# Four-layer cross-attention kernel: the second attention's exponential takes negated maxima as a bias, layer 0's scores use a second ring of banks, and the places of the last layer's stages change

## The reference

```python
# layer 0: per sequence, instance norm, two 64x64 projections, one softmax over the channels' pairs
A  = softmax(Mn^T Mm, axis=-1);  x = Wo (Ml A^T) + bo + x
# layer 1 (the first attention): 32 query heads on 8 key heads, 64 keys, head size 8, additive mask
x  = layernorm(softmax(q k^T / sqrt(8) + mask) v @ Wo + bo + x) * gamma + beta
# layer 2 (the second attention): latents x, keys from context and latents: 128 keys, 16 heads of size 16
a  = softmax(where(mask, q k^T / 16, -inf), axis=-1)
x  = gelu(rmsnorm((a v) @ out_w + out_b + x) @ mlp_w1 + b1) @ mlp_w2 + b2 + x
# layer 3: a recurrent block; per head a state s of 8x8 over 64 time steps, and a channel mix
s  = k_t v_t + w_t * s;  out_t = r_t (u k_t v_t + s)
```

## Time and profile before

| what | value |
|---|---|
| profiled execution, its own time | 1816.85 us |
| its span, first to last instruction | 1815.0 us |
| median of three other executions | 1815.32 us (1812.19 to 1816.52) |
| mean granted TensorE clock | 0.959 of full speed |
| busy: PE, DVE, ACT, POOL | 89%, 67%, 52%, 42% |
| period of a group (group 3's layer 0 to group 4's) | 623.52 to 840.90 us |

### The profile page before, as it was taken

How to read it: one execution, slowest core, us unless ns; L and a number is a source line. 1 busy time by engine, 2 the same in 40 slices (tenths; PEclk the granted TensorE clock), 3 DMA queues, 4 the chain that set the end, 5 groups by cost and what they waited for, 6 DMA issues and landing times.

```text
span 1815.0 us, 35492 instructions
## 1 busy us (share of the span) xinstructions
PE 1621.3 (89%) x13831; PEld 1053.9 (58%) x13831; DVE 1221.7 (67%) x2259; ACT 936.1 (52%) x1922; POOL 770.9 (42%) x882
## 2 busy tenths in 40 slices
PE   5888898899998899998998989889899889988856
PEld 3666556675565655655566655667456565565534
DVE  3743569755786558845689456975579665884496
ACT  4455545555645545556455564555564554555313
POOL 5532248603584046721477024860358404672000
PEclk8999999998999999999999999999999999999978
DMA  6001014210241004310061101421024100520060
GB/s 194 1 2 38 1 18 56 32 36 7 33 58 37 19 1 57 40 30 19 1 72 26 30 20 18 55 34 34 7 35 56 37 20 1 62 36 1 13 90 17
DMA packets 75924, 60.84 MB, mean 34 GB/s; under 512 B 39264, under 2 KB 60912, under 8 KB 75760
## 3 DMA queue, kind: packets, MB, share of 16 engines
q1 hardware_dynamic: 58000, 47.99, 18.3%
q10 hardware_dynamic: 17216, 10.55, 2.1%
q0 software_dynamic: 544, 0.03, 0.0%
HBM read 20.28 MB, written 4.19 MB: 13 GB/s over the span
## 4 chain that ended last, share of the span: by engine, by line
PE 66%; DVE 14%; ACT 9%; issue 5%; POOL 5%; DMA 0%; ACTq 0%; DVEq 0%; SPq 0%; POOLq 0%
PE bank L690 26%; PE bank L834 7%; PE bank L1097 6%; PE bank L1034 5%; DVE late L1409 4%; PE bank L706 3%; PE bank L1059 2%; PE bank L981 2%; ACT soft_ring L1235 2%; PE bank L967 2%; POOL soft_ring L1785 2%; PE bank L1052 2%; PE bank L943 2%; PE bank L954 1%; PE bank L774 1%
## 5 line engine op out<-in xcount | busy, mean ns | idle before, releaser
L1785 POOL TENSOR_TENSOR soft_ring<-soft_ring,seg_max 128x512 f32<-128x512 f32 x256 | 279.5, 1107 | 282.4 <-DVE seg_max L1575 281.4
L1250 ACT ACTIVATE soft_ring<-soft_ring 128x512 f32<-128x512 f32 x256 | 160.1, 625 | 188.1 <-POOL soft_ring L1785 188.0
L1409 DVE TENSOR_TENSOR_SCAN late<-late 128x520 f32<-128x520 f32 (+1 forms) x128 | 211.1, 1649 | 15.8 <-POOL late L1740 12.2
L834 PE MATMUL bank<-early 32*128 32x128 f32 (+2 forms) x1024 | 152.3, 416 | 39.1 <-ACT soft_ring L1235 37.9
L1034 PE MATMUL bank<-ident,soft_ring 128*128 128x128 f32 x1024 | 165.0, 290 | 22.8 <-ACT soft_ring L1250 17.4
L1738 POOL TENSOR_TENSOR late<-late 128x520 f32<-128x520 f32 x112 | 167.9, 1499 | 38.9 <-DVE late L1409 38.5
L1034 PEld LDWEIGHTS bank<-ident,soft_ring 128*128 128x128 f32 x1024 | 116.9, 145 | 92.8 <-ACT soft_ring L1250 44.9
L1575 DVE TENSOR_REDUCE seg_max<-soft_ring 128x8 f32<-128x512 f32 (+1 forms) x256 | 165.5, 674 | 0.2
L1751 POOL COPY late<-edge 128x8 f32<-128x8 f32 (+1 forms) x16 | 3.1, 197 | 327.2 <-DVE late L1513 279.5
L1793 POOL TENSOR_SCALAR soft_ring<-soft_ring,rden 128x256 f32<-128x256 f32 x64 | 59.3, 927 | 180.4 <-DVE rden L1537 180.4
L834 PEld LDWEIGHTS bank<-early 32*128 32x128 f32 (+1 forms) x1024 | 76.7, 192 | 90.0 <-issue 88.0
(11 more groups left out here) (327 smaller groups left out, 3482.2 us busy)
## 6 DMA issues: line engine op xcount, KB each, us to landing
late<-late SPq DMA_DIRECT2D x112, 260.0 KB, 4.4
c<-in_ctx ACTq DMA_DIRECT2D x8, 512.0 KB, 4.1
x<-in_x ACTq DMA_DIRECT2D x8, 512.0 KB, 4.9
out_x<-late SPq DMA_DIRECT2D x7, 512.0 KB, 2.9
late<-late SPq DMA_DIRECT2D x16, 130.0 KB, 3.8
early<-early SPq DMA_DIRECT2D x16, 130.0 KB, 3.6
mask<-in_mask_Bx1xSxS_ff ACTq DMA_DIRECT2D x16, 128.0 KB, 4.0
mask<-in_mask_BxS_ik SPq DMA_DIRECT2D x8, 256.0 KB, 3.5
```

What stands on the lines that cost most here:

```text
L834: ins = mm(t[:, width * n:width * n + width], lhsT, rhs, start=True, stop=True)
L1250: af(soft[:, u % SOFT, :], soft[:, u % SOFT, :], ACT.Exp).then_inc(sig("exp"), 1)
L1409: nc.vector.tensor_tensor_scan(P.sj[:, n % 2, :], P.wP[:, k, :, :].rearrange("p b t -> p (b t)"), P.aj[:, n % 2, :], 0.0, ALU.mult, ALU.ad ...
L1785: tt(s, s, seg_max[:, u % SOFT, 0:segs].unsqueeze(2).broadcast_to([128, segs, 512 // segs]), ALU.subtract).then_inc(sig("sub"), 1)
```

## The change

It has five parts. Maxima of the second attention are written negated, POOL no longer subtracts them, and ACT takes four exponentials of 128 columns with a column of the maxima as bias, in place of one of 512; ACT waits for DVE's "max" where it waited for POOL's "sub". In layer 0 the scores of pairs 1 and 3 go to the ring "turn". The two squares of a half (L1302) are waited for once and not one by one. `PLACES` and `SCAN_PLACES` have new numbers (in the order PE, ACT, DVE, POOL).

```diff
-            "normalize": (4, 12, 1, 0),
-            "turn": (11, 12, 5, 0),
-            "shift": (12, 15, 11, 4),
-            "maa": (15, 16, 12, 12),
-            "mix 0": (17, 29, 16, 18),
-            "mix 1": (22, 29, 20, 18),
+            "normalize": (4, 5, 1, 0),
+            "turn": (11, 10, 3, 0),
+            "shift": (11, 10, 11, 9),
+            "maa": (15, 15, 15, 10),
+            "mix 0": (17, 28, 18, 17),
+            "mix 1": (22, 28, 24, 28),
...
-            "bonus": (56, 49, 54, 56),
-            "center": (124, 124, 121, 113),
-            "variance": (127, 128, 122, 121),
-            "gate": (132, 130, 124, 121),
-            "project": (132, 133, 126, 127),
+            "bonus": (56, 50, 53, 54),
+            "center": (125, 125, 121, 118),
+            "variance": (127, 127, 124, 126),
+            "gate": (130, 129, 124, 126),
+            "project": (133, 133, 124, 126),
...
-            "ffn k": (135, 135, 133, 141),
-            "ffn r": (141, 145, 137, 147),
-            "ffn v": (149, 151, 148, 151),
+            "ffn k": (135, 141, 128, 138),
+            "ffn r": (138, 149, 128, 153),
+            "ffn v": (147, 154, 146, 156),
         }
         SCAN_PLACES = (
-            (64, 53, 64, 60), (64, 53, 68, 63), (64, 54, 68, 66), (64, 59, 69, 67), (72, 59, 69, 67),
-            (78, 78, 69, 67), (78, 80, 70, 67), (84, 88, 84, 70), (85, 91, 88, 89), (98, 93, 88, 89),
-            (101, 93, 100, 89), (107, 93, 105, 100), (112, 94, 108, 105), (116, 94, 109, 107), (116, 97, 114, 109),
-            (116, 107, 117, 109), (116, 109, 117, 109), (116, 111, 119, 111), (122, 114, 121, 111),
+            (63, 52, 64, 58), (63, 54, 67, 65), (64, 54, 67, 66), (65, 61, 67, 67), (71, 61, 69, 67),
+            (75, 79, 69, 67), (75, 79, 71, 67), (83, 89, 83, 67), (83, 90, 88, 85), (96, 93, 88, 89),
+            (100, 93, 100, 90), (105, 99, 106, 100), (109, 100, 108, 105), (112, 102, 109, 105), (112, 102, 115, 105),
+            (112, 106, 117, 105), (116, 107, 120, 110), (116, 110, 120, 110), (125, 115, 121, 110),
         )
...
-                def side_by_side(tiles, steps, operands):
-                    held = [fill(pe, "score", tile) for tile in tiles]
+                def side_by_side(tiles, steps, operands, ring="score"):
+                    held = [fill(pe, ring, tile) for tile in tiles]
...
                     side_by_side([("s0", 2 * p), ("s0", 2 * p + 1)], 2, lambda n, half: (
-                        mn[HALVES[half], p, 128 * n:128 * n + 128], mm0[HALVES[half], p, :]))
+                        mn[HALVES[half], p, 128 * n:128 * n + 128], mm0[HALVES[half], p, :]), "turn" if p % 2 else "score")
...
                 def exps(u):
                     tables(LOG_EXP, TANH)
-                    act.wait_ge(sig("sub"), past("sub") + u + 1)
-                    af(soft[:, u % SOFT, :], soft[:, u % SOFT, :], ACT.Exp).then_inc(sig("exp"), 1)
+                    if u < UNITS:
+                        act.wait_ge(sig("sub"), past("sub") + u + 1)
+                        af(soft[:, u % SOFT, :], soft[:, u % SOFT, :], ACT.Exp).then_inc(sig("exp"), 1)
+                        return
+                    act.wait_ge(sig("max"), past("max") + u + 1)
+                    s = soft[:, u % SOFT, :].rearrange("p (h n) -> p h n", h=4)
+                    for h in range(4):
+                        ins = af(s[:, h, :], s[:, h, :], ACT.Exp, bias=seg_max[:, u % SOFT, h:h + 1])
+                    ins.then_inc(sig("exp"), 1)
...
-                                link(af(xh[:, p, :], xr[:, p, :], ACT.Square, accum_out=stats[:, p, 0:1]))
+                                ins = af(xh[:, p, :], xr[:, p, :], ACT.Square, accum_out=stats[:, p, 0:1])
+                            link(ins)
...
                     nc.vector.tensor_reduce(seg_max[:, u % SOFT, 0:KVH if u < UNITS else 4], cuts(u, soft[:, u % SOFT, :]),
-                                            X, ALU.max).then_inc(sig("max"), 1)
+                                            X, ALU.max, negate=u >= UNITS).then_inc(sig("max"), 1)
...
                 def subtract(u):
                     pool.wait_ge(sig("max"), past("max") + u + 1)
-                    segs = KVH if u < UNITS else 4
-                    s = soft[:, u % SOFT, :].rearrange("p (h s) -> p h s", h=segs)
-                    tt(s, s, seg_max[:, u % SOFT, 0:segs].unsqueeze(2).broadcast_to([128, segs, 512 // segs]),
+                    s = soft[:, u % SOFT, :].rearrange("p (h s) -> p h s", h=KVH)
+                    tt(s, s, seg_max[:, u % SOFT, 0:KVH].unsqueeze(2).broadcast_to([128, KVH, L]),
                        ALU.subtract).then_inc(sig("sub"), 1)
...
-                    if unit(i) >= 0:
+                    if 0 <= unit(i) < UNITS:
                         subtract(unit(i))
```

More of the change, by code:

```diff
@@ L478, in build @@
             "moments": (0, 0, 0, 0),
-            "normalize": (4, 12, 1, 0),
-            "turn": (11, 12, 5, 0),
-            "shift": (12, 15, 11, 4),
-            "maa": (15, 16, 12, 12),
-            "mix 0": (17, 29, 16, 18),
-            "mix 1": (22, 29, 20, 18),
-            "td": (29, 29, 30, 18),
-            "k": (32, 29, 34, 18),
-            "mix 2": (35, 29, 35, 22),
-            "decay": (37, 36, 36, 23),
-            "v": (42, 37, 40, 31),
-            "mix 3": (42, 37, 40, 35),
-            "mix 4": (43, 39, 42, 46),
-            "r": (45, 43, 42, 47),
-            "g": (49, 49, 46, 48),
-            "r u k": (50, 49, 50, 48),
-            "bonus": (56, 49, 54, 56),
-            "center": (124, 124, 121, 113),
-            "variance": (127, 128, 122, 121),
-            "gate": (132, 130, 124, 121),
-            "project": (132, 133, 126, 127),
-            "moments 2": (133, 133, 127, 132),
-            "normalize 2": (133, 133, 128, 133),
-            "turn 2": (134, 133, 130, 134),
-            "shift 2": (135, 135, 133, 140),
-            "ffn k": (135, 135, 133, 141),
-            "ffn r": (141, 145, 137, 147),
-            "ffn v": (149, 151, 148, 151),
+            "normalize": (4, 5, 1, 0),
[4 more added lines that the diff above has]
+            "mix 1": (22, 28, 24, 28),
+            "td": (29, 28, 28, 32),
+            "k": (32, 29, 34, 33),
+            "mix 2": (35, 29, 34, 33),
+            "decay": (39, 36, 37, 36),
+            "v": (42, 36, 41, 37),
+            "mix 3": (42, 36, 41, 39),
+            "mix 4": (43, 39, 42, 50),
+            "r": (46, 43, 43, 50),
+            "g": (49, 49, 46, 50),
+            "r u k": (52, 50, 50, 50),
+            "bonus": (56, 50, 53, 54),
[3 more added lines that the diff above has]
+            "project": (133, 133, 124, 126),
+            "moments 2": (133, 133, 127, 126),
+            "normalize 2": (134, 133, 127, 134),
+            "turn 2": (134, 133, 127, 134),
+            "shift 2": (135, 137, 127, 134),
+            "ffn k": (135, 141, 128, 138),
+            "ffn r": (138, 149, 128, 153),
+            "ffn v": (147, 154, 146, 156),
         }
         SCAN_PLACES = (
[4 rows of a table removed]
[4 rows of a table added]
         )
@@ L530, in build @@
             nmax0_ready=8, over_ready=8, p0_ready=8, p0b_ready=8,
-            rden0_ready=8, rstd0_ready=1, rstd1_ready=2, rstd2_ready=2, stats0_ready=1, stats1_ready=2, sub=32,
+            rden0_ready=8, rstd0_ready=1, rstd1_ready=2, rstd2_ready=2, stats0_ready=1, stats1_ready=2, sub=16,
             v2_zero=1, x0_in=16, xh1_ready=4, xh2_ready=4, xr3_ready=4,
```

## The result

The kernel after takes 1803.57 us (median of 4 executions, 1801.66 to 1805.32), the kernel before 1815.92 us beside it: ratio 0.9935, 95% interval 0.9916 to 0.9954. It is faster by 12 us, half of the 25 us forecast. The profiled execution of after took 1801.66 us, its span is 1799.9 us.

The account below looks back on a forecast made before the run. PE's work (1621.3 us busy) plus its idle time was taken as the bound. 17.6 + 5.4 + 6 - 4 = 25 us off 1816.85 gave 1791.9, as a median 1790.5 us; range 1765 to 1818.

Parts of the forecast that it names:

- The other edits … nothing: Negated maxima, single wait for the squares, new places: almost nothing; up to 1 us per period if one chain is longer.
- Second attention, forecast 5.4 + 6 - 4 = 7.4 us: 5.4 us from waits gone, 6 us from a freed DVE, less 4 us for ACT's longer exponentials.
- the waits of 0.78 us: PE's wait late in the second attention of seven woven periods, from POOL's backlog, taken as gone: 5.4 us.
- ACT's charge, 4 us: Second attention: four exponentials add 0.64 us of ACT's time per unit; 0.5 us per group charged, 4 us in all.
- ACT becomes the bound: Rival, chance 0.12: in each group's second attention PE follows ACT, 41 us on the path; 1838 us.
- Layer 0, forecast 17.6 us: Scores of pair 1 run at once in other banks: 2.2 us less in each of 8 layers 0, bounds 8 to 29.
- about 2 us: Layer 0: idle time that stays in front of PE's first transposition, releaser L1325 or L1793.
- I expect one slow stretch to stay in most layers 0: Layer 0: since about 2 us of idle time stay, the lower clock stays too; nothing counted for it.
- DVE beside a quieter POOL: Second attention: fewer subtractions speed up DVE's scans and reads, for which PE waits; 6 us, bounds 0 and 21.
- Caught at the next stop: Rival, chance 0.14: layer 0 gains, but between the attentions DVE, POOL and the new places cost it again; 1810 us.
- a new long wait at … L774: Sign of being wrong: a new long wait at L880 or L774, which would be the new places' doing; no size given.
- its chances for "faster": Whole kernel: below 1809.9 us, from the forecast, the all-waits-pay rival and half of two others; sum given as 0.76.

Follow-up runs that it names:

- V: The kernel after with ScalarE's place of "variance" put back from 127 to 128: 1795.08 us, 0.9877 of the kernel before.
- a_scan_last12: V with the scan place entries 7 to 18 as in the kernel before, entries 0 to 6 new: 0.9797 of the kernel before.
- b_exps: The kernel before with only the four exponentials and the negated maxima, old banks and places: 1799.47 us, 0.9905 of the kernel before.
- a_oldscan: V with all 19 scan place entries as in the kernel before: 1779.14 us, 0.9794 of the kernel before.
- a_noexp_var: V with the old exponential (one of 512 columns behind POOL's subtraction), new scan places: 1786.51 us, 0.9832 of the kernel before.
- a_pe_7to8: V with TensorE's places of scan entries 7 and 8 moved from 83 and 83 to 84 and 85: 1783.58 us, 0.9818 of the kernel before.
- a_fill: V with one unit's transpositions in each second attention written four times into the same bank: 1780.03 us, 0.9802 of the kernel before.

## Why the forecast got the direction and half the size

- **"The other edits … nothing" is the step that failed.** I looked for waits at the places and found hardly any; I did not ask what each move opens. ScalarE's variance one place earlier costs 8.5 us (V), and the late scan places 15 us (a_scan_last12). Together 24 us; without them the change gives 37 us, more than the 25 forecast. I also took the parts as a sum, each with a worth of its own. They haven't: the scan places cost 15 us with the new exponential and nothing with the old one (0.9832 with the new places, 0.9864 with the old). That 12 us came out, half of the forecast, is a balance of terms that I hadn't counted: these 24 us lost and 12 us more won elsewhere.
- **Second attention, forecast 5.4 + 6 - 4 = 7.4 us.** Its idle time fell by 8.8 us in the second attention proper, so what I counted was there; the waits of 0.78 us are gone. It came to nothing in after because the time at the lower clock rose by 26.8 us. With the old scan places the same part gives 14 to 17 us (b_exps; a_oldscan against its like without it): there it isn't given back. That this is twice the forecast's 7.4 is not to the forecast's credit: in both pairs the clock adds its part, which I hadn't counted.
- **ACT's charge, 4 us.** The durations held: 391 ns where I had about 400, and four in 1.26 us where I had 1.3. The charge came at one place that I hadn't named. ACT in group 3, after:

```profile
730.54 1.26 ACT L1256 ACTIVATE soft_ring<-soft_ring,seg_max 128x128 f32<-128x128 f32 x4
731.70 0.57 ACT L1266 ACTIVATE early<-bank 128x512 f32<-128x512 f32 x1
732.18 1.26 ACT L1256 ACTIVATE soft_ring<-soft_ring,seg_max 128x128 f32<-128x128 f32 x4
733.35 0.58 ACT L1266 ACTIVATE early<-bank 128x512 f32<-128x512 f32 x1
733.83 1.00 ACT L1288 ACTIVATE hT<-bank,vec 128x256 f32<-128x256 f32 x2
```

  hT's copy stands behind two units' exponentials and copies, and PE's wait for it is 24.2 us with the new exponential, 11.2 with the old (a_noexp_var). In itself that is the mechanism of the rival "ACT becomes the bound", at a third of its price; ACT's fullest stretch held PE up in the first period alone, by 2.73 us once.
- **Layer 0, forecast 17.6 us, came out at 23.6** by the profiles. The first transposition waits 2.38 us, as forecast ("about 2 us"), with POOL's scaling as the releaser. The idle time gave 9.4 us. The rest is the clock, which I took as unchanged ("I expect one slow stretch to stay in most layers 0"): of eight layers 0 five now have none, where before all had some. And the credit isn't the bank change's alone: by itself it gives 0, and 12 us with VectorE's "mix 0" behind the last maximum, one of the edits that I costed at nothing.
- **DVE beside a quieter POOL**, forecast 6 us: the scans fell from 1649 to 1531 ns as a mean, the reads from 777 to 670, together 29 us of DVE's time, more than the 21 that I took as the whole excess (b_exps, with the old places, has 1572 and 653 ns, 26 us). The credit doesn't show where I placed it: PE's waits for the reads grew from 17.9 to 29.1 us, and were 16.6 with the old scan places (a_oldscan), 1.3 below before. DVE's own saving was underestimated and PE's share of it overestimated; for these reads DVE is waited for by its order, not by its speed.

The rival that came nearest is "Caught at the next stop" (1810): 13.7 us more idle time between the attentions. Of the new waits there 8.5 us are the new places' (1.22 us for a read, L774, in each woven period); the wait for hT takes the new exponential as well. This is also the one sign of being wrong that came, "a new long wait at … L774", beside those of being right. The rival too left out the clock. One sum of the prediction is slightly off: its chances for "faster" add up to 0.775, not 0.76.

## What to carry to other kernels

Read the granted clock stretch by stretch beside the idle time. A wait of 2 us on TensorE can have a second price, the lower clock behind it, and it is due where the slow matmuls fall: under a wait they cost next to nothing (0.2 us in group 3 of a_pe_7to8), in a busy stretch half their time. Where an order of work is tuned, a change of one part is to be timed with the old and with the new order; here the same edit saved 17 us or cost 10, by the order around it.

## What the hardware showed that was not expected

- Repeating 12 transpositions in a gap, 1.3 us of useless matmuls in each of eight periods, made the kernel 15 us faster (0.9877 to 0.9802). The Trainium skill ("TensorE: Matmul & The Clock Gate", section "A second HAM failure mode: psum-queue depth-cycling") says that frequent short idle times between groups of matmuls make the clock swing between its two levels. These traces agree: with idle times of 2.3 to 2.7 us, once or twice in a second attention, 36.6 us stand at the lower clock, and 4.8 where the woven periods have none above 1.7 us.
- The same idle time doesn't always bring the lower clock. V has the wait for hT in every period, and the period at 941.80 still ran its second attention at 1.00. What else it takes stays open.
- Within the 64-column matmuls (L1059) TensorE stands still for up to 2.7 us for no reason that the trace shows ("issue", at 761.71 in V), in before too. In a_fill, with 24 more instructions ahead of it on TensorE (transpositions and weight loads), it stands at another place and is shorter. Where it comes from wasn't tried.
- A load of a function table took 1.28 us on ScalarE.
